# Edge aggregation with alpha-scaled one-hots as the moving operand: sums come out channel by node, and the last stage drops its transposes

## The reference, cut to what matters

```python
alpha = jax.nn.softmax(a, axis=0)                 # over all edges, per head
alpha_mean = alpha.mean(axis=1, keepdims=True)
agg = jax.ops.segment_sum(msg * alpha_mean, dst, num_segments=node_features.shape[0])
out = node_features + agg @ W_out
mu = out.mean(axis=-1, keepdims=True)
var = out.var(axis=-1, keepdims=True)
return (out - mu) / jnp.sqrt(var + EPS)
```

## Time and profile before

| | us |
|---|---|
| median of 3 runs | 3501.98 |
| the three runs | 3501.98, 3503.55, 3498.74 |
| span of the profiled execution | 3499.8 |
| busy in it: PE, PEld | 2791.7, 1977.5 |
| busy in it: DVE, ACT, POOL | 2528.0, 2041.3, 2085.4 |
| loop over items in `layer1_aggregate`, first to last DVE addition start | 3111.8 to 3437.8 |
| `finish`, from its first DMA to the end | 3438.4 to 3499.8 |

### The profile page before, as it was taken

The page is one execution under the profiler, slowest core; times in us unless marked ns, Lnnn a source line. Parts: engine busy times, 40 slices in busy tenths (PEclk is TensorE's granted clock), DMA queues, the critical chain, the costliest instruction groups (busy, mean ns, idle before and its releaser), DMA issues. The chain is left out here.

```text
span 3499.8 us, 76247 instructions
## 1 busy us (share of the span) xinstructions
PE 2791.7 (80%) x17156; PEld 1977.5 (57%) x17380; DVE 2528.0 (72%) x4445; ACT 2041.3 (58%) x4527; POOL 2085.4 (60%) x2160
## 2 busy tenths in 40 slices
PE   1577777777777777744799999999999999958885
PEld 0355555555555555532466666666666666647774
DVE  5699999999999999996345555555554555567776
ACT  6355555555555555545355555555555555568885
POOL 0177777777777777732777777777777777500001
PEclk9899999999999999978899999999999999989997
DMA  2555444554444444413777777777777777647662
GB/s 71 172 143 145 142 142 141 142 144 144 142 139 141 143 141 143 141 34 106 206 218 222 218 218 221 220 218 221 217 222 220 220 220 218 190 132 202 202 202 82
DMA packets 391734, 595.68 MB, mean 170 GB/s; under 512 B 73317, under 2 KB 237855, under 8 KB 391682
## 3 DMA queue, kind: packets, MB, share of 16 engines
q0 software_dynamic: 98304, 268.57, 27.1%
q1 hardware_dynamic: 242626, 247.55, 25.4%
q10 hardware_dynamic: 50752, 78.99, 6.6%
HBM read 501.15 MB, written 93.68 MB: 170 GB/s over the span
## 5 line engine op out<-in xcount | busy, mean ns | idle before, releaser
L1194 POOL DMA_INDIRECT l_G<-rows_d,l_sidx x1024 | 1002.5, 979 | 363.1 <-issue 276.3
L807 POOL DMA_INDIRECT l_G<-rows_d,l_sidx x1024 | 1014.0, 990 | 330.5 <-issue 305.0
L1322 ACT ACTIVATE l_h<-l_H,l_cols 128x512 f32<-128x512 f32 x512 | 350.7, 685 | 557.3 <-PE l_H L1229 540.5
L875 PE MATMUL l_accp<-l_we,l_ohe 128*128 128x256 f32 x2048 | 486.3, 380 | 0.0
L831 PE MATMUL l_A<-ident,l_G 128*128 128x128 f32 x1024 | 172.8, 293 | 380.6 <-DVE l_oht L978 323.0
L1386 DVE TENSOR_TENSOR big<-l_SC,l_b 128x512 f32<-128x512 f32 x256 | 177.1, 692 | 387.9 <-PE l_SC L1258 387.9
L875 PEld LDWEIGHTS l_accp<-l_we,l_ohe 128*128 128x128 f32 x2048 | 371.1, 191 | 40.1
L831 PEld LDWEIGHTS l_A<-ident,l_G 128*128 128x128 f32 x1024 | 111.2, 144 | 482.0 <-issue 243.5
L1258 PEld LDWEIGHTS l_SC<-big,l_h 128*128 128x128 f32 x2048 | 263.6, 191 | 146.8 <-issue 146.8
L1548 PE MATMUL ag_accp<-ag_msg,ag_pick 128*128 128x128 f32 x2048 | 286.5, 288 | 73.7 <-ACT ag_msg L1532 32.9
L903 ACT ACTIVATE l_qe<-l_A 128x512 f32<-128x512 f32 x256 | 153.3, 599 | 325.8 <-PE l_A L834 209.7
(11 more groups left out here) (182 smaller groups left out, 5755.4 us busy)
## 6 DMA issues: line engine op xcount, KB each, us to landing
msg_d<-l_msg ACTq DMA_DIRECT2D x256, 256.0 KB, 2.2
ag_msg<-msg_d SPq DMA_DIRECT2D x256, 256.0 KB, 2.9
l_G<-rows_d,l_sidx POOLq DMA_INDIRECT x2048, 3.3
l_lo<-mark_d SPq DMA_DIRECT2D x256, 128.0 KB, 3.0
l_lo<-code_d SPq DMA_DIRECT2D x256, 128.0 KB
l_in<-in_ea_dram SPq DMA_DIRECT2D x512, 64.0 KB
l_fd<-dst_d SPq DMA_DIRECT2D x256, 96.0 KB, 3.4
l_pd<-dst_d SPq DMA_DIRECT2D x256, 96.0 KB
```

The costliest lines, as they stand in the source:

```text
L807: nc.gpsimd.indirect_dma_start(out=G[:, s, j, :], out_offset=None, in_=rows_d[0][:, :], in_offset=bass.IndirectOffsetOnAxis(ap=sidx[:, hal ...
L875: last = nc.tensor.matmul(accp[b][:, 0:2 * C], oh_e[:, b, j, :], we_t[:, b, j, :], start=(j == 0), stop=(j == TJ - 1), skip_group_check=True)
L1194: nc.gpsimd.indirect_dma_start(out=G[:, s, j, :], out_offset=None, in_=rows_d[1][:, :], in_offset=bass.IndirectOffsetOnAxis(ap=sidx[:, hal ...
L1322: nc.scalar.activation(out_t[:, s % 2, :], in_p[:, :], ACT.Silu, bias=cols[:, col:col + 1]).then_inc(ready, 1)
```

## The change

In the aggregation, four DVE instructions per item, one for each tile, make a one-hot that carries alpha: (column number equals local node number) times alpha. Both per-edge values are per-partition operands with addresses that depend on the item. ACT no longer scales messages, nor does DVE; PE waits for the load itself. PE takes the unscaled message as stationary and the alpha-carrying one-hot as moving operand, so that the sum in `acc1` is channel by node. In `finish`, `acc1` goes straight into the product with `W_out` as stationary operand; the turns and ACT's copies are gone, and `pp` has four buffers in place of two.

```diff
 # layer1_aggregate, ACT
-                            act.wait_ge(ld[s], 16 * (lp + 1))
-                            for j in range(TJ - OWN[s], TJ):
-                                mine = msg_t[:, s, j, :]
-                                nc.scalar.activation(mine, mine, ACT.Copy,
-                                                     scale=al[:, bass.ds(i * TJ + j, 1)]).then_inc(shared, 1)
-                        run_items(act, step)
 # layer1_aggregate, PE
-                            pe.wait_ge(shared, lp * SHARED[-1] + SHARED[s])
-                            pe.wait_ge(pick_ready, lp * PICKED[-1] + PICKED[s])
+                            pe.wait_ge(ld[s], 16 * (lp + 1))
+                            pe.wait_ge(pick_ready, i + 1)
                             if after(i, R):
                                 pe.wait_ge(acc_done, i - R + 1)
                             for j in range(TJ):
-                                last = nc.tensor.matmul(accp[b][:, :], pick[:, b, j, :], msg_t[:, s, j, :],
+                                last = nc.tensor.matmul(accp[b][:, :], msg_t[:, s, j, :], pick[:, b, j, :],
                                                         start=(j == 0), stop=(j == TJ - 1))
 # layer1_aggregate, DVE, weigh
-                            nc.vector.tensor_tensor(pick[:, b, :, :], iota_row[:, :].unsqueeze(1).to_broadcast([P, TJ, P]),
-                                                    local[:, bass.ds(i * TJ, TJ)].unsqueeze(2).to_broadcast([P, TJ, P]),
-                                                    ALU.is_equal).then_inc(pick_ready, 1)
-                            if OWN[s] == TJ:
-                                return
-                            dve.wait_ge(ld[s], 16 * (lp + 1))
-                            mine = msg_t[:, s, 0, :]
-                            nc.vector.tensor_scalar(mine, mine, al[:, bass.ds(i * TJ, 1)], None,
-                                                    ALU.mult).then_inc(pick_ready, 1)
+                            for j in range(TJ):
+                                last = nc.vector.tensor_scalar(pick[:, b, j, :], iota_row[:, :],
+                                                               local[:, bass.ds(i * TJ + j, 1)], al[:, bass.ds(i * TJ + j, 1)],
+                                                               ALU.is_equal, ALU.mult)
+                            last.then_inc(pick_ready, 1)
 # finish, PE
-                        turn(0)
-                        for g in range(HALF):
-                            turn(g + 1)
-                            pe.wait_ge(s_at, g + 1)
-                            if g >= 2:
-                                pe.wait_ge(s_sum, g - 1)
+                        for g in range(HALF):
+                            if g >= 4:
+                                pe.wait_ge(s_sum, g - 3)
                             for k in range(2):
-                                last = nc.tensor.matmul(pp[g % 2][:, k, :], a_t[:, g % 2, k, :], w_o[:, :], start=True, stop=True)
+                                last = nc.tensor.matmul(pp[g % 4][:, k, :], acc1[:, (2 * g + k) * C:(2 * g + k + 1) * C], w_o[:, :],
+                                                        start=True, stop=True)
 # finish, ACT
-                            if g < HALF:
-                                act.wait_ge(s_tp, g + 1)
-                                if g >= 2:
-                                    act.wait_ge(s_pp, g - 1)
-                                nc.scalar.activation(a_t[:, g % 2, :, :], tp[g % 2][:, :, :], ACT.Copy).then_inc(s_at, 1)
 # finish, DVE
-                                nc.vector.tensor_tensor(mine, mine, pp[g % 2][:, :, :], ALU.add).then_inc(s_sum, 1)
+                                nc.vector.tensor_tensor(mine, mine, pp[g % 4][:, :, :], ALU.add).then_inc(s_sum, 1)
```

More of the change, by code:

```diff
@@ L1465, in layer1_aggregate @@
             T = NI * TJ
-            OWN = [TJ - 1 + s % 2 for s in range(U)]
-            SHARED = [sum(OWN[0:s + 1]) for s in range(U)]
-            PICKED = [sum(1 + TJ - n for n in OWN[0:s + 1]) for s in range(U)]
             st = ExitStack()
@@ L1490, in layer1_aggregate @@
                 s_alpha = sem("ag_alpha_ready", st)
-                shared = sem("ag_shared", st)
                 pick_ready = sem("ag_pick_ready", st)
@@ L1620, in finish @@
                 w_o = sb("fi_w", [P, C], F32, st)
-                a_t = sb("fi_at", [P, 2, 2, C], F32, st)
                 stats = sb("fi_stats", [P, 4, NBT], F32, st)
                 O = sb("fi_O", [P, NBT, C], F32, st)
-                tp = [ps(f"fi_tp{k}", [P, 2, C], F32, st) for k in range(2)]
-                pp = [ps(f"fi_pp{k}", [P, 2, C], F32, st) for k in range(2)]
+                pp = [ps(f"fi_pp{k}", [P, 2, C], F32, st) for k in range(4)]
                 s_in = sem("fi_in", st)
@@ L1637, in finish @@
                 s_root = sem("fi_root", st)
-                s_tp = sem("fi_tp_ready", st)
-                s_at = sem("fi_at_ready", st)
                 s_pp = sem("fi_pp_ready", st)
@@ L1665, in _ @@
                         pe.wait_ge(s_in, 16)
-                        def turn(g):
-                            if g >= HALF:
-                                return
-                            if g >= 2:
-                                pe.wait_ge(s_at, g - 1)
-                            for k in range(2):
[L1673 to L1676, removed]
-                        turn(0)
-                        for g in range(HALF):
-                            turn(g + 1)
-                            pe.wait_ge(s_at, g + 1)
-                            if g >= 2:
-                                pe.wait_ge(s_sum, g - 1)
-                            for k in range(2):
-                                last = nc.tensor.matmul(pp[g % 2][:, k, :], a_t[:, g % 2, k, :], w_o[:, :], start=True, stop=True)
+                        for g in range(HALF):
+                            if g >= 4:
+                                pe.wait_ge(s_sum, g - 3)
+                            for k in range(2):
+                                last = nc.tensor.matmul(pp[g % 4][:, k, :], acc1[:, (2 * g + k) * C:(2 * g + k + 1) * C], w_o[:, :],
+                                                        start=True, stop=True)
                             last.then_inc(s_pp, 1)
```

## The result

| | before | after |
|---|---|---|
| median, us | 3500.73 (4 runs) | 3619.03 (4 runs) |
| span of the profiled execution, us | 3499.8 | 3611.5 |
| first to last start of the 256 additions, us | 326.0 | 450.0 |
| from the last addition's start to the end, us | 62.0 | 54.9 |

The ratio is 1.0334, with a 95% interval of 1.0319 to 1.0348: 118 us slower. Forecast were 3575 us and a range of 3540 to 3660. The two stages account for it: 450.0 - 326.0 = +124.0 and 54.9 - 62.0 = -7.1, together +117. (The spans differ by only 112 us because the profiled execution after happened to reach the first addition 5.2 us earlier. That point, in front of everything the change touches in the loop, lies between 3106.6 and 3115.9 us in the ten profiles of this study.)

What follows compares the result with a forecast made beforehand. DVE's sequencer was taken to bound the aggregation loop. Terms: +80 one-hots, -5 load wait, +4 datapath, -6 finish, +73 on a span of 3499.8, 3573; the median lies 2.2 above, so 3575 us, range 3540 to 3660.

Steps and rivals of the forecast that it cites:

- DVE's sequencer sets the pace, and computed addresses are what costs: Aggregation loop: DVE's sequencer, not its datapath, sets the pace; one more instruction with a register-computed address costs it 0.15 us.
- The price of a one-hot: DVE's sequencer in the loop: 0.14 us per new one-hot, a step of 1.50 us against 1.165, +80 us over 240 items.
- rival 1: DVE's sequencer in the loop: two register instructions per one-hot, step 1.94 us, 3681 us; chance 0.15 including values between.
- the forecast's case: Aggregation loop: prices of 0.12 to 0.17 us per one-hot, 3548 to 3605 us; chance 0.72.
- 0.94 us for the rest of the step: DVE's step in the loop without the one-hots: load, addition and waits, 1.09 - 0.15 = 0.94 us.
- The laps: Aggregation loop, per lap of eight items: the branch and other register work cost about 0.9 us before the change.
- Rival 2: DVE's steps in the loop: sequencer runs ahead, datapath sets 1.22 us, 3481 us; break-even about 0.07 us per one-hot; chance 0.06.
- Datapath 1.22 us, hidden: DVE's datapath: four one-hots at 0.256 us and an addition make 1.22 us, hidden in the loop; +4 us in written-out items.
- Operands exchanged at no cost, ACT and SP off the path: Aggregation: PE's exchanged operands, ACT's lost scalings and SP's loads each change the time by 0.
- Finish -6: Last stage: 10.6 us of DVE's waits for products go, two more slow small products add 2 x 2.3; net -6 us.
- Rival 3: PE in the aggregation: the clock falls to its lower level, an item takes 2.1 us, 3706 us if it stayed; chance 0.04.

## Why the prediction was right, and where it was off

- *DVE's sequencer sets the pace, and computed addresses are what costs*: right. Fixed addresses remove 141 us, taking other register work from the same chain removes 74, and the datapath was idle 0.33 us or more before nearly every addition, as foretold.
- *The price of a one-hot*: mis-sized, and with it the sum. I took 0.14 us, from register instructions of 46 to 65 ns, where two addresses in one instruction take 93 ns. With the additional 40 ns instruction in seven items of eight a one-hot costs (1.70 - 0.94) / 4 = 0.19 us. About 0.10 of that is in the register rows; no row shows the rest, and it is worked out with the 0.94. The step was 1.70, not 1.50; 240 x 0.20 = 48 us, where the median missed by 44. So the measured time lies outside the 3548 to 3605 us that I gave a chance of 0.72, and in the part between that case and rival 1 that I gave 0.15. (The lower edge is mis-summed: a price of 0.12 gives 3575 - 960 x 0.02 = 3556.) It lies between the two cases that I had weighed: the addresses are packed into one instruction, which rival 1 doubted, but the instruction is longer. The run with one fixed address, at 3576 us, is the forecast's case.
- *0.94 us for the rest of the step*: not measured by itself. The run with one fixed address has steps of 1.50 to 1.51 us, as 0.94 + 4 x 0.14 says, but that checks only the sum of the two.
- *The laps*: I took the mean of 1.278 us for the loop's, though the faster written-out items count in it. A lap before was 10.40 us (one-hots behind the branch at 3337.51 and 3347.91 us), so the branch and the rest took 1.08 us, not 0.9. After, they take 14.44 - 8 x 1.70 = 0.84, where I had 0.75. Over 30 laps the loop grew by 121 us where I had 75, and the written-out items by 3 where I had 4. Rival 2's break-even price also comes out at 0.061 us from its own numbers, not 0.07. Neither slip moved the forecast by more than a few us.
- *Datapath 1.22 us, hidden*: right, shown by two runs at 1.22 and 1.23. The Trainium skill (VectorE: DVE Perf Modes, the section on the TRN2 errata) gives 58 cycles plus elements over speed-up; for a 128-element float32 operation at double rate I estimate 127 ns from it. The runs show 0.256 us between starts with DVE fully busy, twice that, so the measurement decides against it for an instruction with two per-partition operands.
- *Operands exchanged at no cost, ACT and SP off the path*: right.
- *Finish -6*: it gave 7.1, by the two steps named. 11.2 us of waits for products went (14.0 to 2.8; forecast 10.6), and 3.8 came back in the small product (forecast 4.6). On this the Trainium skill (SBUF — State Buffer, the section Who interferes with whom) says that a VectorE instruction with two SBUF inputs contends with a GpSimd instruction that reads SBUF; the trace agrees, with 2.5 to 2.8 us for a product of ten columns while POOL's addition of 2.88 us runs, and 0.17 us for the one that meets none.
- *Rival 2, faster with the sequencer ahead*: it became true in exactly the runs that took the addresses away, with 1.22 us as worked out. The 3481 us given for it are the 3478 and 3484 measured.
- *Rival 3, the clock*: it did dip, to 0.93 in the window from 3150 to 3200 us, which I had named as a sign of being wrong. It did not decide: that window and the one from 3250 to 3300 us, at 1.00, each hold 28 additions, and DVE hardly waited for PE (3.6 us in all).

Open: why the 40 ns instruction appears in seven items of each lap's eight (it is not there with one address fixed; no run changed it alone), and what the part of a one-hot's price is that no register row shows.

## What to carry to other kernels

When a loop's engines all show slack and one has short idle times marked "issue" before the same instruction, add up its sequencer's rows. Here an instruction with one computed address costs the issuing engine's sequencer 0.14 to 0.15 us, one with two 0.19, and a checked register load with the addition behind it 0.94 (all worked out from differences of steps), and they are serial. Before splitting one instruction into four, compare the period of the same step written out with constants and inside the loop (1.22 and 1.70 us here): the difference is the sequencer's work that the datapath does not cover. The address arithmetic can be moved to an idle engine that copies the operands to fixed places, and a bounds check in such a chain (0.29 us per item in the changed kernel) is the first thing to weigh.

## What the runs showed that was not expected

- Ahead of a one-hot, the register instruction takes 65 ns (57 to 75) with one computed address and 93 ns with two.
- The end of a lap costs 0.84 us in the changed kernel, 0.46 of it as one idle time of DVE. It vanishes when DVE's datapath is the bound (50.00 of 50 us busy, laps of 9.79 us, eight steps of 1.22 to 1.23).
- Leaving out one bounds check in the kernel with the old one-hots takes the additions from 1.279 to 1.020 us apart, and the loads go from 203 to 258 GB/s with no change to them.
